# Softmax weights kept in fp32 and streamed past a narrow stationary operand, with the attention heads placed anew around a recurrence

## What is computed

```python
q, k, v = (_to_heads(plin(xm, w, b)) for w, b in ((w_q, b_q), (w_k, b_k), (w_v, b_v)))
qt, kt, vt = (logmap0(q), logmap0(k), logmap0(v))
scores = jnp.einsum('bhqd,bhkd->bhqk', qt, kt) / math.sqrt(HD)     # HD = 16, 16 heads
attn = jax.nn.softmax(scores, axis=-1)
out_h = expmap0(jnp.einsum('bhqk,bhkd->bhqd', attn, vt))
attn_out = plin(_from_heads(out_h), w_o, b_o)
...
ff = plin(plin(xm, w_f1, b_f1), w_f2, b_f2)
...
def step(carry, xw_t):          # 512 steps, xw_t = x @ Wx + b
    prev_h, prev_c = carry
    a = xw_t + prev_h @ Wh
    ...
    next_c = f * prev_c + i * g
    next_h = o * jnp.tanh(next_c)
```

## Time and profile before

| | us |
|---|---|
| three runs | 1553.27, 1553.42, 1554.94 |
| median | 1553.42 |
| the profiled execution | 1551.88 |
| its span, first to last instruction | 1550.0 |

### The profile page before, as it was taken

The page is one execution under the profiler, slowest core; times in us unless marked ns, Lnnn a source line. Parts: engine busy times, 40 slices in busy tenths (PEclk is TensorE's granted clock), DMA queues, the critical chain, the costliest instruction groups (busy, mean ns, idle before and its releaser), DMA issues.

```text
span 1550.0 us, 65350 instructions
## 1 busy us (share of the span) xinstructions
PE 1418.1 (91%) x25395; PEld 1205.5 (78%) x25395; DVE 1159.0 (75%) x6593; ACT 913.9 (59%) x3340; POOL 466.3 (30%) x1230
## 2 busy tenths in 40 slices
PE   3786854799999999999999999999999999999998
PEld 3674543688888888888888888888888888888886
DVE  5898763688887878788878787877676676766665
ACT  2687952767766676767675767574545444444433
POOL 2453120043251515151515151515131322220000
PEclk9997556799999999999999999999999999999999
DMA  8000000000000000000000000000000000000000
GB/s 267 6 1 1 1 1 1 5 3 3 10 3 10 3 10 3 10 3 10 3 10 3 10 3 10 3 10 3 10 3 9 3 10 3 6 3 6 3 7 5
DMA packets 16718, 18.48 MB, mean 12 GB/s; under 512 B 6036, under 2 KB 15384, under 8 KB 16408
## 3 DMA queue, kind: packets, MB, share of 16 engines
q1 hardware_dynamic: 13016, 10.51, 2.3%
q10 hardware_dynamic: 3392, 3.81, 1.0%
HBM read 12.21 MB, written 2.10 MB: 9 GB/s over the span
## 4 chain that ended last, share of the span: by engine, by line
PE 62%; DVE 24%; ACT 6%; issue 6%; POOL 1%; DMA 1%; DVEq 0%; ACTq 0%; POOLq 0%
PE psum L784 26%; PE psum L823 17%; PE psum L759 3%; PE psum L659 3%; PE psum L724 3%; DVE cnew L1522 2%; ACT ot L1045 2%; DVE weights L1273 2%; DVE hl L1531 2%; DVE hl L1529 2%; PE psum L731 2%; PE psum L739 2%; PE psum L774 2%; PE psum L671 2%; DVE gO L1517 1%
## 5 line engine op out<-in xcount | busy, mean ns | idle before, releaser
L784 PEld LDWEIGHTS psum<-hl,wh 128*128 128x128 f16 x16384 | 470.6, 96 | 80.7 <-DVE hl L1531 72.7
L784 PE MATMUL psum<-hl,wh 128*128 128x8 f16 x16384 | 515.4, 172 | 15.2 <-DVE hl L1531 6.2
L823 PE MATMUL psum<-zeros,ident 128*128 128x256 f16 (+2 forms) x3374 | 415.7, 263 | 7.3 <-DVE gF L1515 2.0
L823 PEld LDWEIGHTS psum<-zeros,ident 128*128 128x128 f16 x3374 | 308.0, 98 | 78.8 <-DVE gF L1515 17.2
L1039 ACT ACTIVATE tA<-gA 128x16 f32<-128x16 f32 x512 | 110.5, 216 | 427.2 <-DVE gA L1513 426.7
L1273 DVE TENSOR_TENSOR weights<-w,weights 128x256 f16<-128x256 f32 x512 | 202.7, 418 | 15.0 <-ACT weights L940 14.8
L1513 DVE TENSOR_REDUCE gA<-psum 128x16 f32<-128x32 f32 x512 | 96.3, 188 | 126.1 <-PE psum L784 118.9
L1529 DVE TENSOR_TENSOR hl<-ot 128x8 f16<-128x8 f32 x512 | 89.9, 176 | 95.1 <-ACT ot L1045 94.1
L946 ACT ACTIVATE w<-psum 128x512 f32<-128x512 f32 x256 | 154.3, 603 | 5.6 <-DVE weights L1273 4.5
L1045 ACT ACTIVATE ot<-cnew 128x8 f32<-128x8 f32 x512 | 109.7, 214 | 81.0 <-DVE cnew L1522 29.8
L940 ACT ACTIVATE weights<-psum 128x512 f16<-128x512 f32 x256 | 153.6, 600 | 3.9 <-PE psum L671 3.9
(11 more groups left out here) (299 smaller groups left out, 2207.5 us busy)
## 6 DMA issues: line engine op xcount, KB each, us to landing
arena<-in_x_dram SPq DMA_DIRECT2D x4, 512.0 KB, 9.1
wf<-in_L_cond_w_f_dram SPq DMA_DIRECT2D x2, 1024.0 KB, 20.0
xr<-in_x_dram SPq DMA_DIRECT2D x64, 32.0 KB, 1.9
out_dram<-place SPq DMA_DIRECT2D x64, 32.0 KB, 1.6
qTs<-in_L_cond_w_ada_dram ACTq DMA_DIRECT2D x1, 1536.0 KB
oT<-in_L_cond_Wh_dram ACTq DMA_DIRECT2D x1, 1024.0 KB, 12.6
wx<-in_L_cond_Wx_dram SPq DMA_DIRECT2D x1, 1024.0 KB, 16.6
rows<-in_L_cond_b_ada_dram ACTq DMA_DIRECT2D x4, 128.0 KB, 14.9
```

The lines of the kernel that those rows point to most:

```text
L784: last = mm(cols, wh16[:, half, kc, (g0 + c) * P:(g0 + c + 1) * P], hl[:, :, kc, :, 2].rearrange("p e b -> p b e"), start=False, stop=c == ...
L823: mm(pF[:, D:D + n], ident16[:], zeros[:, 0:n], start=False, stop=False, skip_group_check=True)
```

## The change

- **Exponentials.** ACT takes one exponential a head, in fp32, into `w32`, which has 8 buffers instead of 4. The second exponential, the subtraction on DVE and the fp16 `weights` go. ACT waits for the weighted product of 8 heads before.
- **Values.** `vs` is fp32 with 17 columns a head (16 and the constant). `values` on POOL has two operations fewer.
- **Weighted product.** It is issued 3 slots behind the scores, with operands exchanged: `vs` (128x17 fp32) is stationary, and `w32` moves, 128 fp32 columns, 4 matmuls a head. The head's 17 outputs come out on partitions 32 (h mod 4) and up. Where the heads lie ahead of the steps (`batched`), four heads are issued together, 16 matmuls that take turns over the four groups of partitions.
- **Turning back.** Behind a tile's last head ACT copies the bank to `oc`, PE turns it with four fp32 transposes (`turned_back`) and DVE reads it once a tile (two operations instead of two per 8 heads). DVE clears the bank once, ahead of all.
- **Places.** Block 1's heads lie in slots -82 to -19. Blocks 2 and 3 lie in windows of 32 slots, 16 heads in each, at ranks 0, 2, 4, 6 and 10 to 21, in slots 31 to 148 and 159 to 276.
- **Merging.** `settle(k)` is 13 for tiles 0 to 7 and 17 for the later ones, and some of the small steps come 2 or 3 ranks earlier for those.
- **Filler.** `beside` books 1024 columns for a weighted product, 256 for scores and 512 for a turning back; `EARLY` goes; the raised steps are 0 to 3 and 23, 87, 151, 215, 279.

```diff
-SETTLE = 13
+SETTLE = (13, 17)
...
-BESIDE, EARLY, RAISE, HEADS_END = 2640, 2900, 4500, 300
+BESIDE, RAISE, HEADS_END = 2640, 4500, 330
+BEFORE_STEPS = -82
+WINDOWS = (3, 7)
+WINDOW_RANKS = (0, 2, 4, 6) + tuple(range(10, 22))
...
-    return (FIRST + i, -19 + i, 46 + 2 * i, 174 + 2 * i)[block]
+    if block < 2:
+        return (FIRST, BEFORE_STEPS)[block] + i
+    return RING * (WINDOWS[block - 2] + i // H) - PAUSE + WINDOW_RANKS[i % H]
...
+def batched(n):
+
+    return head_slot(n // 4 * 4 + 3) < 0
...
-                vh, vl = (vs[:, k % B, k // B, :, i * (HD + 1):i * (HD + 1) + HD] for i in range(2))
-                g.tensor_tensor(v32, lin_of(k)[:, 2, :].rearrange("p (h e) -> p h e", e=HD),
+                g.tensor_tensor(vs[:, k % B, k // B, :, 0:HD], lin_of(k)[:, 2, :].rearrange("p (h e) -> p h e", e=HD),
                                 num("fv", H).unsqueeze(2).to_broadcast([P, H, HD]), ALU.mult).then_inc(s["p_v"], 1)
-                hold(pool, "p_v", k + 1)
-                g.tensor_copy(vh, v32).then_inc(s["p_vh"], 1)
-                hold(pool, "p_vh", k + 1)
-                g.tensor_tensor(vl, v32, vh, ALU.subtract).then_inc(s["p_vl"], 1)
...
-            def weighted(m):
-
-                k, h = m // H, m % H
-                pe.wait_ge(s["t_l"], 2 * m + 2)
-                if m % 8 == 0 and m > 0:
-                    pe.wait_ge(s["t_u"], m // 8)
+            def weighted(first, last):
+
+                k = first // H
+                pe.wait_ge(s["t_e"], last + 1)
+                if first % H == 0 and k >= 1:
+                    pe.wait_ge(s["t_u"], k)
                 for kc in range(NB):
-                    for wl in range(2):
-                        last = mm(pV[:, h % 8 * W1:(h % 8 + 1) * W1], weights[:, m % 4, wl, kc * P:(kc + 1) * P], vs[:, k % B, kc, h, :],
-                                  start=kc == 0 and wl == 0, stop=kc == NB - 1 and wl == 1, skip_group_check=True)
-                last.then_inc(s["t_AV"], 1)
+                    for m in range(first, last + 1):
+                        h = m % H
+                        done = mm(pV[32 * (h % 4):32 * (h % 4) + HD + 1, h // 4 * P:(h // 4 + 1) * P], vs[:, k % B, kc, h, :],
+                                  w32[:, m % 8, kc * P:(kc + 1) * P], start=kc == 0, stop=kc == NB - 1, skip_group_check=True)
+                done.then_inc(s["t_AV"], last + 1 - first)
+
+            def turned_back(k):
+
+                pe.wait_ge(s["t_c"], k + 1)
+                for i in range(4):
+                    last = tr(pV[:, i * P:(i + 1) * P], oc[:, i * P:(i + 1) * P], ident[:])
+                last.then_inc(s["t_T"], 1)
...
-                if t - 5 in HEAD_AT:
-                    weighted(HEAD_AT[t - 5])
+                m = HEAD_AT.get(t - 4, 0)
+                if m % H == H - 1:
+                    turned_back(m // H)
+                if t - 3 in HEAD_AT:
+                    m = HEAD_AT[t - 3]
+                    if not batched(m):
+                        weighted(m, m)
+                    elif m % 4 == 3:
+                        weighted(m - 3, m)
...
-                cols = 264 * (t - 5 in HEAD_AT) + 256 * (t in HEAD_AT) + 256 * (t % RING == 4 and t > RING) + 2048 * ((t + 1) % ROUND == 0)
+                cols = 1024 * (t - 3 in HEAD_AT) + 512 * (HEAD_AT.get(t - 4, 0) % H == H - 1) + 256 * (t in HEAD_AT) + 256 * (t % RING == 4 and t > RING) + 2048 * ((t + 1) % ROUND == 0)
...
-                wanted = RAISE if t < 4 or t % 64 in (0, 1) and t < HEADS_END else BESIDE if t >= 2 * RING else EARLY
+                wanted = RAISE if t < 4 or t % 64 == 23 and t < HEADS_END else BESIDE
...
-                if t - 1 in HEAD_AT:
-                    m = HEAD_AT[t - 1]
-                    if m >= 4:
-                        act.wait_ge(s["t_AV"], m - 3)
-                    A(weights[:, m % 4, 0, :], bank[m % 2], ACT.Exp, scale=1.0 / (math.sqrt(HD) * QK_UP * QK_UP)).then_inc(s["t_e"], 1)
+                m = HEAD_AT.get(t - 3, 0)
+                if m % H == H - 1:
+                    act.wait_ge(s["t_AV"], m + 1)
+                    if m // H >= 1:
+                        act.wait_ge(s["t_T"], m // H)
+                    A(oc, pV, ACT.Copy).then_inc(s["t_c"], 1)
                 if t in HEAD_AT:
                     m = HEAD_AT[t]
                     act.wait_ge(s["t_S"], m + 1)
-                    if m >= 4:
-                        act.wait_ge(s["t_l"], 2 * m - 6)
-                    A(w32[:, m % 4, :], bank[m % 2], ACT.Exp, scale=1.0 / (math.sqrt(HD) * QK_UP * QK_UP)).then_inc(s["t_E"], 1)
+                    if m >= 8:
+                        act.wait_ge(s["t_AV"], m - 7)
+                    A(w32[:, m % 8, :], bank[m % 2], ACT.Exp, scale=1.0 / (math.sqrt(HD) * QK_UP * QK_UP)).then_inc(s["t_e"], 1)
...
-            def low_weights(m, half):
-
-                part = slice(half * T // 2, (half + 1) * T // 2)
-                v.wait_ge(s["t_e"], m + 1)
-                d.tensor_tensor(weights[:, m % 4, 1, part], w32[:, m % 4, part], weights[:, m % 4, 0, part], ALU.subtract).then_inc(s["t_l"], 1)
```

More of the change, by code:

```diff
@@ L101 @@
 PM_ORDER = [use for slot, rank, use in sorted(
-    [(merged_slot(k) + SETTLE, 0, ("merged", k)) for k in range(NT)] +
+    [(merged_slot(k) + settle(k), 0, ("merged", k)) for k in range(NT)] +
     [(RING * n - PAUSE + 1, 2, ("rows", n)) for n in range(NT)] +
@@ L199, in bass_hyperbolic_block_then_lstm @@
         tmp = sb("tmp", [P, FF])
+        oc = tmp[:, 0:T]
         xn = sb("xn", [P, D])
@@ L690, in merged @@
             def merged(k, r):
[L692 removed]
+                if r == settle(k):
                     pe.wait_ge(s["m_oS"], k + 1)
@@ L1252, in _ @@
                 between_turns(turn)
+            d.memset(bank[2], 0.0)
             v.wait_ge(s["h0p"], 4)
```

59 lines of the change are left out of this document (23 added, 36 removed).

## The result

| | before | after |
|---|---|---|
| median, us (runs beside each other) | 1554.09 (4 runs, 1553.27 to 1554.94) | 1573.14 (4 runs, 1562.34 to 1576.88) |
| the profiled execution | 1551.88 | 1571.85 |
| its span | 1550.0 | 1570.1 |

The ratio is 1.0111 (95% interval 1.0060 to 1.0162): the changed kernel is slower by 19 us, or 1.1%. (Where some runs of a kernel are more than 1.5% longer than its fastest, ratios and intervals here are taken without them.) The four runs of after are spread over 14.5 us, and their mean granted clocks, 0.973, 0.966, 0.962 and 0.958, stand in the order of their times, the fastest run first.

What follows compares the result with a forecast made beforehand. In the steps the recurrence sets a 2.318 us floor, and PE sets the period where its other work is longer. 1551.9 + 27 (steps) - 4.5 (ahead of them) = 1574.4, 1576 on the median's scale; range 1532 to 1618.

Steps and rivals of the forecast that it cites:

- The steps: The 511 periods between cell updates: 83 us over the floor against 55 before, a loss of 27 us.
- ranks 7 and 9: Steps of a 32-step window with a weighted product and line 739's chunk: 2.73 us each, 0.82 a window over the floor.
- The 16 us of waits between engines: Steps before the change: 55 us over the floor against 39 summed; left out, but the range widened by 8 upwards.
- The price of the product: A head's new weighted product on PE in a step: 0.96 us, 0.76 more than before, bounds 0.43 and 1.15.
- Rival 2: In the steps, the narrow product costs only the 1024 columns booked, 0.43 us: kernel 1530 us; chance 0.10.
- The set-up: Before the first scores: nothing taken for the two dropped POOL operations, between -2 and +1 us.
- Block 0: First block's 64 heads, ahead of the steps: 65 us against 67.0, -2, with a batch of four at 1.75 us.
- Rival 1: Ahead of the steps, column groups overlap fully, a batch takes 1.0 us: -36 us there, kernel 1544; chance 0.20.
- The 17 heads and the chain: Second block's heads before and within row tile 0's chain, ahead of the steps: +1.5 and +9.5 us.
- rival 4: Ahead of the steps, exponentials stand behind the chain's waits on ACT: chain 60 us, kernel 1583; chance within the forecast's 0.55.
- The last 19 slots: Just before step 0, without their heads: 20 us instead of 33.7, -13.5.
- rival 3: Ahead of the steps, batches don't overlap or the clock stays low: +45 to +53 us there, kernel 1627; chance 0.15.

Runs made afterwards that it cites:

- the repeated run: The changed kernel run again with nothing altered, beside the first experiments: 1569.64 us beside 1553.59, ratio 1.0114.

## Why the prediction was right, and where only the sum was

The forecast was 1576 us, the result 1573.14: slower, by about what was said. Part of that is luck, as errors of both signs met.

**The steps** were argued rightly: +21.4 where +27 stood. Both products in a step 2.83 us, as predicted to the hundredth; rank 16 3.21 (3.32); ranks 22 and 23 2.60 (2.64), 24 2.76 where it isn't raised (2.64); ranks 3 and 5 2.70 and 2.81 (2.64). The filler did not give way, and booking it made these steps 0.5 us shorter. The term that was mis-sized is ranks 7 and 9: 2.73 forecast, 2.37 and 2.32 measured, 0.8 us a window and 6 in all, about the whole difference; smaller misses (ranks 3 and 5 above, rank 16 and others below) cancel. The sum took the column sums and the head's product one after the other, but they go to different column groups; the run with the sums at partition 96 brought rank 9 back up. The 16 us of waits between engines that today's steps had over their sum did not stay: with ranks 7 and 9 put right, the row-by-row sum gives 77 us over the floor, and 76 were measured.

**The price of the product** held: 0.98 us for 0.96 forecast from line 739. Rival 2, 0.43 us, is out. On drains: the product starts 0.93 us behind the gate products, full-width work 0.87, so a change of shape costs no more than 0.06.

**The set-up** was the largest miss: 0 forecast, -11.4 measured. The step that failed was "POOL is not the busy engine, so I take nothing". The bound of -2 was argued from shares, and the way by which a POOL operation costs DVE time was not looked for. Its trace was at hand: line 1211 takes 885 ns where its twin in the same turn takes 666, and each starts just behind a POOL operation.

**Block 0** gained 9.8 us, not 2. Timeline of PE in after, a batch at the lower clock and one at the upper:

```profile
150.17 1.91 PE L676 MATMUL psum<-w,vs 128*17 128x128 f32 x32
152.01 0.50 PE L663 MATMUL psum<-qTs,kT 64*128 64x128 f16 x3
...
176.82 1.07 PE L676 MATMUL psum<-w,vs 128*17 128x128 f32 x32
177.82 0.41 PE L663 MATMUL psum<-qTs,kT 64*128 64x128 f16 x8
```

32 records take 1.84 us and 1.00 to the next group: 1.00 is the lower bound of the forecast, at which only issue counts, where 1.75 was taken because two records of one matmul go to the same group. 3.44 / 1.00 is a factor of 3.4 for four groups. The Trainium skill, TensorE: Matmul & The Clock Gate, Measured speedup vs the span model, gives 2.38 for three; the 1.45 us that the prediction worked out from it was too dear as well. That column tiles overlap, as its figure says, this trace shows. Rival 1 was thus right on its mechanism, and did not come about. One reason is the clock, which it took to be at its upper level: it was 0.68 in block 0. Over the profiles of this placement without filler ahead, block 0 took 52.4 us with 14.5 us at the lower clock and 65.0 with 56.1; a straight line through the two gives 48 with none, an estimate, near rival 1's 49. The other reason lies in the chain and the last slots, below. A cycle of four heads was 4.15 us at the lower and 2.90 at the upper, 3.55 forecast.

**The 17 heads and the chain** lost 25.7 us where +11 stood. The 17 heads took 1.25 us each, with PE busy in 17.6 of 21.2 us at 0.64 of the clock; the forecast had 0.89, at the upper clock. That miss is the clock: in the eight other profiles without filler ahead this stretch ran at the upper clock and took 16.1 us each time, 0.95 a head. From the repeated run:

```profile
191.80:207.90 16.10, 12.23 (x253) 8.26 (x249) 3.78 (x17) 12.51 (x25) 3.43 (x2) 1.00 0.01 2
```

The chain took 59.2 for 53, and here the clock is not the reason: over these nine profiles it took 59.2 to 60.4 us with 18.8 to 30.7 us at the lower clock, in no order, and with filler 64.2 and 64.3. So it is 6 us longer than the forecast at either share of the clock, and filler makes it longer still. In after PE is busy for 82% of it (48% before); of its 10.5 us of idle time 4.4 end with an exponential of ACT (line 966) and 3.3 with the chain's scaling on ACT (line 1019). Exponentials in the chain's way on ACT, as rival 4 had it, would look like this, but no run took them apart.

**The last 19 slots** took 27.8 for 20 forecast. The heads are gone from them, and the next late thing is row tile 0's own chain (timeline of PE, idle time in brackets):

```profile
287.78 0.69 PE L767 MATMUL psum<-ident,X 128*128 128x128 f32 x2 [7.53 <-DVE X L1517]
```

PE stands 7.5 us for it. In the ten other profiles of this placement this stretch is 27.4 to 28.0 us as well, so the 20 were too few. What sets it stays open: in all eleven the clock was at its lower level for 17.1 us of it, and no run put filler or anything else there.

**Sum of the misses** against the forecast: set-up -11.4, block 0 -7.8, 17 heads +8.5, chain +6.2, last slots +7.6, steps -5.6: -2.5 in all, out of 47 in absolute size (42 by lengths, where block 0 is -5.5 and the 17 heads +6.2). The range held them; the forecast time came so near because they met. Two of the rivals' sums were also slightly off, without effect: rival 2's 37 - 55 is -18, not -19, and rival 3's middle is 1629, not 1627.

## What to carry to other kernels

Narrow stationaries pay when their outputs are spread over column groups and issued in turns: four fp32 products of 17 columns took the time of one. With batches in the steps, the filler booked anew, the heads moved and filler ahead, a loss of 1.1% became a gain of 2.3%; the batches themselves brought the kernel from 1.0010 to 0.9932. When real work replaces filler, cut the filler by the time that the work takes, but look at the granted clock after it, in all runs and not only in the profiled one, for the filler may be what keeps it up. And an engine that is mostly idle can still hold another one: look at the durations of the same operation beside and away from the idle engine's work, not at shares.

## What the hardware showed that was not expected

- DVE operations that started just behind a POOL operation ended 0.26 to 0.28 us behind its end (885 and 666 ns for 418 and 425), a cast 0.15 us (715 ns for 290) and a copy 0.08 us (715 for 220): in each case its own length less some 0.15 us.
- fp32 matmuls to four column groups overlap, two records each and all: 32 records in 1.00 us, which is what the 32 records of the gate products take too, against 0.107 us a record on one group. It holds between instructions of different widths too (17 and 1 columns).
- A busy PE did not keep its clock: it fell to its lower level behind 20.26 us in which PE was busy for 19.43, and stayed there for 17.07 us with PE busy in all of them. Scores and products had taken the filler's place in these steps. With 256 columns more of filler booked beside the scores, 58.0 us at the lower clock in the profiled steps became 3.4. Which mix of work makes it turn is not settled.
